# Second attention of a two-layer kernel: half of the query splits moved from VectorE to GpSimd, the output bias moved with them, the quotients left in PSUM

## What is computed

```python
x = x + _L1_xattn_ref(_layernorm(x), ctx_1024, ctx_1024, W_q, b_q, W_k, b_k, W_v, b_v, W_o, b_o)

def _L1_xattn_ref(query, key, value, W_q, b_q, ...):
    Q = query @ W_q.T + b_q          # 16 heads of 8
    K = key @ W_k.T + b_k
    V = value @ W_v.T + b_v
    scores = einsum('bhqd,bhkd->bhqk', Q, K) / sqrt(8)
    attn = softmax(scores)           # over the 64 keys of the own batch
    context = einsum('bhqk,bhkd->bhqd', attn, V)
    output = context @ W_o.T + b_o
```

## Time and profile before

| what | value |
|---|---|
| median of 3 runs | 254.26 us (252.09 to 254.91) |
| the profiled execution, its own time | 256.51 us |
| its span | 254.6 us |
| mean granted TensorE clock | 0.951 |
| busy: PE, DVE, ACT, POOL | 207.9, 191.0, 140.9, 136.3 us |

### The profile page before, as it was taken

How to read it: one execution, slowest core, us unless ns; L and a number is a source line. 1 busy time by engine, 2 the same in 40 slices (tenths; PEclk the granted TensorE clock), 3 DMA queues, 4 the chain that set the end, 5 groups by cost and what they waited for, 6 DMA issues and landing times.

```text
span 254.6 us, 5870 instructions
## 1 busy us (share of the span) xinstructions
PE 207.9 (82%) x2010; PEld 143.0 (56%) x2010; DVE 191.0 (75%) x510; ACT 140.9 (55%) x240; POOL 136.3 (54%) x174
## 2 busy tenths in 40 slices
PE   8979898787999996875678587979976469999970
PEld 3426696443555564453457484756744248888760
DVE  7673648868888887879968999799797176776655
ACT  2132247749544455248876876866864146656650
POOL 7628961232987869478334543951786600255540
PEclk9999999968999999999777979999999979999999
DMA  6900543010021201903000000031001150001124
GB/s 228 393 20 3 146 95 124 0 32 3 1 63 33 62 0 45 279 23 134 10 0 3 1 4 0 11 115 45 4 0 34 54 142 20 13 33 43 35 82 124
DMA packets 12889, 15.63 MB, mean 61 GB/s; under 512 B 1744, under 2 KB 9808, under 8 KB 12736
## 3 DMA queue, kind: packets, MB, share of 16 engines
q1 hardware_dynamic: 10736, 12.77, 16.4%
q0 software_dynamic: 736, 1.53, 1.8%
q10 hardware_dynamic: 1392, 1.00, 1.2%
HBM read 11.18 MB, written 3.06 MB: 56 GB/s over the span
## 4 chain that ended last, share of the span: by engine, by line
PE 45%; DVE 27%; issue 10%; ACT 6%; DMA 4%; POOL 3%; another core or an unknown queue 3%; SPq 1%; DVEq 0%; POOLq 0%; ACTq 0%
DMA attention_or_experts<-ctx_v 4%; PE ps L1641 3%; PE ps L1425 3%; PE ps L1427 3%; PE ps L1426 3%; DVE attention_or_experts L1000 3%; DVE keys_or_scores L1009 3%; PE ps L1576 2%; PE ps L1626 2%; DVE rmax L995 2%; POOL rstd L408 2%; PE ps L1578 2%; PE ps L1577 2%; PE ps L1340 2%
## 5 line engine op out<-in xcount | busy, mean ns | idle before, releaser
L744 ACT ACTIVATE ps<-ps 128x512 f32<-128x512 f32 x47 | 27.5, 584 | 34.1 <-PE ps L1560 19.8
L1188 DVE SCALAR_TENSOR_TENSOR attention_or_experts<-ps,attention_or_experts 128x512 f16<-128x512 f32 x47 | 31.6, 683 | 6.2 <-ACT attention_or_experts L749 5.8
L1576 PE MATMUL ps<-keys_or_scores,attention_or_experts 128*128 128x128 f16 x128 | 23.9, 223 | 11.1 <-DVE attention_or_experts L1188 7.2
L561 POOL DMA_INDIRECT slots_y<-kM,kS x15 | 14.4, 957 | 30.1 <-DVE kM L1211 29.4
L749 ACT ACTIVATE attention_or_experts<-ps 128x512 f16<-128x512 f32 x47 | 27.8, 593 | 0.0
L531 POOL TENSOR_TENSOR attention_or_experts<-attention_or_experts 128x1024 f16<-128x1024 f32 x8 | 17.0, 2128 | 18.2 <-ACT attention_or_experts L708 18.2
L1577 PE MATMUL ps<-keys_or_scores,attention_or_experts 128*128 128x128 f16 x128 | 23.9, 224 | 0.0
L1278 PE MATMUL ps<-idle 128*128 128x512 f16 x82 | 20.8, 402 | 3.8 <-ACT kT L592 1.6
L1578 PE MATMUL ps<-keys_or_scores,attention_or_experts 128*128 128x128 f16 x128 | 23.9, 223 | 0.0
L1576 PEld LDWEIGHTS ps<-keys_or_scores,attention_or_experts 128*128 128x128 f16 x128 | 12.9, 101 | 16.8 <-issue 13.0
L655 ACT ACTIVATE attention_or_experts<-ps 128x512 f32<-128x512 f32 x18 | 10.7, 597 | 19.2 <-PE ps L1427 19.2
(11 more groups left out here) (250 smaller groups left out, 691.1 us busy)
## 6 DMA issues: line engine op xcount, KB each, us to landing
raw<-w_second SPq DMA_DIRECT2D x5, 512.0 KB, 3.7
raw<-w_first SPq DMA_DIRECT2D x9, 192.0 KB, 2.4
raw<-w_second SPq DMA_DIRECT2D x6, 256.0 KB, 2.9
attention_or_experts<-ctx_v SPq DMA_DIRECT2D x1, 1056.0 KB, 9.3
slots_x<-kS SPq DMA_DIRECT2D x1, 990.0 KB, 6.5
kS<-slots_x SPq DMA_DIRECT2D x3, 264.0 KB, 3.4
rw<-rows ACTq DMA_DIRECT2D x1, 512.0 KB, 6.7
ctxT<-ctx_t SPq DMA_DIRECT2D x1, 512.0 KB, 6.8
```

The lines of the kernel that those rows point to most:

```text
L744: a.activation(up_bank(n), up_bank(n), ACT.Gelu, scale=1 / (XS * XS)).then_inc(s["gelu"], 1)
L1188: v.scalar_tensor_tensor(elo[:, n % 4, :], up_bank(n), HS, ehi[:, n % 4, :], ALU.mult, ALU.subtract)\
L1576: mm(o, ehi[:, n % 4, ts], we[:, e, FC + c, 0, :], start=(c == 0 and t == 0), stop=False, skip_group_check=True)
```

## The change

- **Queries of chunks 2 and 3.** ACT moves each piece, with its bias, in float32 from PSUM to a new buffer `qf` in SBUF (`move_queries`; same size as `query_high`). POOL makes both parts from `qf` (`query_parts`: one instruction of 128 x 512 to float16, one of 64 x 512). It does so behind `plo` of tiles 0 to 3, one piece each. `qf` holds one chunk, so the pieces of chunk 3 are moved when those of chunk 2 have been split. DVE's four `query_low` of these chunks go.
- **Banks.** `qbank` is now 6, 7 for chunk 0, 4, 5 for chunk 1, 6, 7 for chunk 2 and 7 for chunk 3. The scores of tile 1 no longer wait for the low part of chunk 1. PE's query products stand in other rounds. The transposes ahead of the second half use bank 2.
- **Output bias.** Added on POOL, ahead of `split_expert(3, (0,))`; `split_expert(3, (1,))` moves behind `plo` of tile 4.
- **Quotients.** `divide` writes to free columns of `values_bank` in PSUM, and `negative_part` and `numbers_only` read them there. The products that write this bank next wait for `o1_ready` (from `numbers_only`) in place of `mul1` (from `divide`) for tiles 6 and 7 and for `up1(2)`.
- **Order.** `sums_of_weights(0)` stands behind `subtract_largest(3)`.

```diff
         def qbank(c, jj):
-            return (4, 5, 2, 3)[2 * c + jj] if c < 2 else 7
+            return (6, 7, 4, 5, 6, 7, 7, 7)[2 * c + jj]
...
# POOL
             split_expert(2, (1,))
-            split_expert(3)
+            def add_output_bias(g):
+                pool.tensor_tensor(xr[:, gt(g), :], xr[:, gt(g), :], pc("bo").unsqueeze(1).to_broadcast([P, TG, E]), ALU.add)\
+                    .then_inc(s["bo_added"], 1)
+            def query_parts(c, jj):
+                m = 2 * (c - 2) + jj
+                js, cs = slice(2 * jj, 2 * jj + 2), slice(c * Q4, (c + 1) * Q4)
+                pool.wait_ge(s["q_moved"], 2 * m + 2)
+                pool.tensor_scalar(qS[:, js, cs], qf[:, js, :], 1.0, 1.0, ALU.mult, ALU.mult).then_inc(s["q_high"], 1)
+                pool.wait_ge(s["q_high"], m + 1)
+                pool.tensor_tensor(qS[S:P, js, cs], qf[S:P, js, :], qS[S:P, js, cs], ALU.subtract).then_inc(s["qS_late"], 1)
+                pool.wait_ge(s["qS_late"], m + 1)
+            for g in range(G):
+                add_output_bias(g)
+            split_expert(3, (0,))
...
                 pool.tensor_tensor(plo[:, t % 2, :], prob[:, t % 2, :], phi[:, t % 2, :], ALU.subtract).then_inc(s["plo_ready"], 1)
+                if t < 4:
+                    query_parts(2 + t // 2, t % 2)
+                if t == 4:
+                    split_expert(3, (1,))
...
# ACT
+            def move_queries(c, jj):
+                a.wait_ge(s["qproj"], 2 * c + jj + 1)
+                if c == 3:
+                    a.wait_ge(s["qS_late"], jj + 1)
+                for j in range(2 * jj, 2 * jj + 2):
+                    a.activation(qf[:, j, :], bank(qbank(c, jj))[:, (j % 2) * Q4:(j % 2 + 1) * Q4], ACT.Identity, bias=bqs[:, j:j + 1])\
+                        .then_inc(s["q_moved"], 1)
             for i in range(NT):
-                if i < 4:
-                    query_high(2 + i // 2, i % 2)
...
+                if i in (2, 3):
+                    move_queries(3, i - 2)
                 exp_scores(i)
+                if i == 0:
+                    for jj in range(2):
+                        move_queries(2, jj)
...
# DVE
-                    last = v.tensor_tensor(o1[q, :, :].rearrange("p (c d) e -> p c d e", d=2), ov[:, :, :, 0:8],
+                    last = v.tensor_tensor(quotients(t)[q, :].rearrange("p (c d e) -> p c d e", d=2, e=D1), ov[:, :, :, 0:8],
...
-                v.tensor_scalar(o1n[:], o1[:], 0.0, None, ALU.min).then_inc(s["min1"], 1)
+                v.tensor_scalar(o1n[:].rearrange("p h d -> p (h d)"), quotients(t), 0.0, None, ALU.min).then_inc(s["min1"], 1)
...
-                v.scalar_tensor_tensor(o1c[:, t % 2, :], o1[:].rearrange("p h d -> p (h d)"), 0.0,
+                v.scalar_tensor_tensor(o1c[:, t % 2, :], quotients(t), 0.0,
...
-                if i in (1, 2):
-                    add_output_bias(i - 1)
+                if i == 3:
+                    sums_of_weights(0)
...
-                if i < 4:
-                    query_low(2 + i // 2, i % 2)
...
# PE
             def scores1(t):
-                pe.wait_ge(s["qS_ready"], 8 if t == 1 else 4 * (t // 2 + 1))
+                if t < 4:
+                    pe.wait_ge(s["qS_ready"], 4 * (t // 2 + 1))
+                else:
+                    pe.wait_ge(s["qS_late"], 2 * (t // 2 - 1))
...
-                    pe.wait_ge(s["mul1"], 5 if t == 6 else 7)
+                    pe.wait_ge(s["o1_ready"], 5 if t == 6 else 7)
```

More of the change, by code:

```diff
@@ L982, in _ @@
             ln_stats(2, 1)
-            def add_output_bias(g):
-                v.wait_ge(s["xn_ready"], 2 * G + g + 1)
-                stat(v.tensor_tensor(xr[:, gt(g), :], xr[:, gt(g), :], pc("bo").unsqueeze(1).to_broadcast([P, TG, E]), ALU.add))
             def scores_of(t):
@@ L1481, in query_products @@
                 pe.wait_ge(s["xT_ready"], 2 * G + c // 2 + 1)
-                if c >= 2:
-                    if (c, jj) != (2, 0):
-                        pe.wait_ge(s["qS_ready"], 4 * c + 2 * jj)
+                if c == 2:
+                    pe.wait_ge(s["qS_ready"], 2 * jj + 2)
+                if c == 3:
+                    pe.wait_ge(s["q_moved"], 4 + 2 * jj)
                 for j in range(2 * jj, 2 * jj + 2):
@@ L1491, in _ @@
                 query_products(0, jj)
-            transpose_norm(2, 1, 6)
+            transpose_norm(2, 1, 2)
+            query_products(1, 0)
             pe.wait_ge(s["kM_ready"], 5)
@@ L1647, in _ @@
                 scores1(i)
[L1648 removed]
+                if i == 1:
+                    query_products(1, 1)
                     for jj in range(2):
[L1650 to L1652 removed]
+                        query_products(2, jj)
                 if i >= 3:
@@ L1658, in _ @@
                     transpose_weights(i - 2, 0)
+                if i in (2, 3):
+                    query_products(3, i - 2)
                 if i == NT - 1:
```

23 lines of the change are left out of this document (13 added, 10 removed).

## The result

The changed kernel takes 247.06 us (median of 5, 246.42 to 252.50) against 254.72 for the kernel before (median of 5). The ratio of the times is 0.9717, 95% interval 0.9653 to 0.9782: 2.8% faster. Executions of every kernel here come in a fast state and in one some per cent slower (of the changed kernel 252.50, the first profiled one, whose granted clock was 0.53 between 19 and 37 us, far ahead of the change, and 252.36), and the ratio compares fast ones only.

What follows compares the result with a forecast made beforehand. DVE was taken to bound the loop, with room on POOL. The terms, -6.0 + 0.8 + 0.2 + 0.8 - 1.8 - 0.6 = -6.6 us, took the profiled 256.5 to 249.9; less 2.2 of scatter, median 247.7, range 245.3 to 251.4.

Steps and rivals of the forecast that it cites:

- start of the loop: `largest` of tile 0, where the second attention's loop begins, stays at 112.82 us: no change.
- part 1: First four tiles, `largest` 0 to 4: DVE loses four `query_low` pieces and two biases, -6.0 us.
- Part 2: Tile 4 to 5: DVE waits 1.1 us for the first output product, behind ACT's late `oT` copy, +0.8 us.
- Part 3: Tiles 5 to 7: DVE-bound as before at 4.36 us a tile, `negative_part` slightly slower from PSUM, +0.2 us.
- part 4: TensorE's clock in the loop: holes between 116 and 124 us bring a stretch at 1.2 GHz, +0.8 us.
- part 5: End of the loop: `numbers_only(4)`, reading PSUM, no longer lies behind POOL's `plo`, so `low_x` comes earlier, -1.8 us.
- part 6: Expert steps 0 to 3: two more quotient rows unblocked, less a partly hidden new wait of `weighted_values(7)`, -0.6 us.
- A: Rival: GpSimd paces the loop if its 64-partition subtraction costs 2.13 us; -4.6 us, 249.7, chance 0.10.
- B: Rival: gains at the loop's end and in the expert steps don't pass on; -4.2 us, 250.1, chance 0.10.
- C: Rival: slower, as holes on PE keep the loop at 1.2 GHz; 257.4 us with five slow intervals, chance 0.04.
- D: Rival: ACT, POOL and the first output product's wait replace more of DVE's time in the loop; -2.6 us, 251.7, chance 0.06.

Runs made afterwards that it cites:

- the first group: Four runs on one chip beside the kernel before: changed kernel again (246.37 us), quotients back in SBUF (250.45), only quotients in PSUM (254.06), only queries moved (250.36).
- the late sum: Changed kernel with `add_attention` and `x_stats` moved behind `numbers_only` in rounds 4 to 6: 247.37 us, ratio 0.9831 to the kernel before.
- experiment 6: Changed kernel with the rounding in `query_parts` made three times over, so GpSimd works longer: 250.28 us, ratio 0.9917 to the kernel before.

## Why the prediction was right

The time (247.7, measured 247.06) and the sign were right, and the mechanism of the largest term was. The closeness of the number is in part luck, as the sum and the split of the parts below show. Its terms, against the second profile of the changed kernel and the first of before:

| term | predicted | measured |
|---|---|---|
| start of the loop | 0 | +0.55 |
| part 1, 0 to 4 | -6.0 | -5.5 (-6.0 in the first profile, clock 1.00) |
| parts 2 and 3, 4 to 7 | +1.0 | +1.5 (+0.8 in the first profile) |
| part 4, the clock | +0.8 | in the two rows above: +0.5 and +0.7 |
| part 5, end of the loop | -1.8 | -1.8 |
| part 6, expert steps | -0.6 | -0.1 |
| sum | -6.6 | -5.4 |
| what only the first profile of before had | | -4.9 |

**Part 1** was walked through step by step and each step came: `subtract_largest(3)` waits 1.21 us for `plo` 1 (1 was said), the parts for tile 4 end at 126.55 (126.3), `largest` 4 is 14.96 behind `largest` 0 (14.5). GpSimd's unseen instruction, the 64 x 512 subtraction, takes 1.15 to 1.16 and the rounding 0.61 to 0.63, both as taken. What the sum credited to VectorE's lighter load is less plain, though. With the quotients in SBUF the piece is 16.14: 1.7 of the 6.0 is there only since the quotients can't be held up by a busy GpSimd. The prediction had this in its sum without knowing it, because it took the quotient of tile 0 as unblocked and looked for collisions only in the rows of before, where GpSimd idles. The times split the same way: in the first group, by the means behind the ratios, the queries take off 3.0 us, the bias 0.2 and the quotients in PSUM, last, 4.0. The sum had 4.4 for the first two together (parts 1, 2 and 4) and 2.2 for the quotients (parts 3, 5 and 6). The total came out right with the split wrong.

**Part 2** sized the wait for the first output product at 1.1; it is 0.64 there and 0.52 for the next tile. `largest` 4 to 5 takes 5.36, 0.4 more than before's 4.95 where 0.8 was said. That both are waits for a product that comes late, and which could have been put off, the late sum shows: they vanish.

**Part 3** was sized too small. A tile that waits for nothing takes 4.57 or 4.58 us, not 4.36 + 0.07. `negative_part` is 0.29 for 0.21 and `numbers_only` stays at 0.29, as taken; `divide` is 0.03 longer. The other 0.11 is in the gaps, which the durations don't show: ahead of `divide` and of `negative_part` they grow by 0.12 and 0.11, ahead of `largest` they shrink by 0.12. The Trainium skill (VectorE: DVE Perf Modes, The TRN2 errata) was nearer in the sum, with 0.13 a tile as an estimate against 0.22 measured, and not in the place: no run shows `numbers_only` slower from PSUM.

**Part 4**: the clock fell from 124 on, behind the holes that the prediction had named, and twice more. There the query product of L1518 took 2.02 us (1.08 at 1.00 in the first profile) and VectorE waited 0.42 for the scores of tile 4. The 1.2 us of the table (by `low_x`, 38.78 against 37.80, 1.0) is the difference of two profiles of the changed kernel. The 0.8 was meant beyond what the kernel before pays, and that isn't shown: read microsecond by microsecond, an estimate, the first profile of before spent about 13.6 us of its loop at the lower level, the two of the changed kernel 10.3 and 6.8.

**Part 5** has the right size, for a reason that was half right. That `numbers_only(4)` was held by `plo` 7, and isn't from PSUM, holds. But PSUM quotients alone leave `low_x` where it was, since `plo` 7 then holds up `ln_apply`, whose operands are in SBUF, and the kernel before gets the same 1.9 us by the order of `plo` 7 alone. In the changed kernel `plo` 7 begins just as `ln_apply` ends. The Trainium skill (SBUF — State Buffer, the two separate sides) has VectorE instructions in a 2-port mode take part in the exclusion too. The trace agrees so far that `ln_apply`, with one tensor input, was held (2.96 beside a `plo` of 2.12); whether it ran in such a mode no run shows. The prediction quoted that rule and looked for it in the rows of the quotients only.

**Part 6** is the term that failed. It took the new wait of `weighted_values(7)` as partly hidden. On TensorE the up products on either side of it stand 2.99 us apart (157.01 and 160.00) where they stood 1.92 apart (161.94 and 163.86): 1.1 us, paid in full.

```profile
159.40 0.18 PE L1570 MATMUL ps<-v1hi,attention_or_experts 128*128 128x36 f16 x1 [0.90 <-DVE o1c L1081]
```

On VectorE, from `low_x` to the placing of the rows, the balance is 0.1 us gained of the 0.6. The two free rows give 0.7 from start to start. A third row, which the prediction didn't name, gives 0.6: a `tensor_scalar` of the router took 1.08 before (L1077, at 168.71, and it ended with a GpSimd subtraction) and takes 0.51. Against this the first output product comes 0.3 later and the waits behind the late values take 0.8.

**Before's own time**: the prediction took the 2.2 us of the profiled execution above the median as scatter. It was a single 4.9 us wait that others don't have, while others have losses that this one hadn't (in the second profile the loop starts 1.5 later and the first output product behind it comes 3.1 later). That the terms give 5.4 and the ratio 7.2 us is not resolved; a part of it may be that such losses are rarer in the changed kernel, which no run here tests. So 247.7 came from a sum that was 1.2 too large by these rows and from a start that was set by 2.2 us of scatter in place of a wait of 4.9, and it met the measured time partly by luck.

Rivals: A is near (experiment 6) and didn't come, as GpSimd's price was the one taken. B came in half, for part 6. C and D didn't come: `largest` 4 to 7 takes at most 15.18, and the clock was back at 1.00 between the stretches.
